# A gated cross-attention mix and a mixture of eight experts on one core: moving the first expert's weights into earlier tiles, a second early pair, and a shift made by ScalarE

## What is computed

```
si, sj = ctx @ Wi, ctx @ Wj                              # one number per row each
mix    = 0.6 * sigmoid(si[:, None] + sj[None, :] + b) + 0.4 * layernorm(x)
x      = x + tanh(g_xattn) * mix
h      = layernorm(x)
probs  = softmax(h @ wg)                                 # 8 experts
e      = argmax(probs)                                   # one expert per row
x      = x + tanh(g_ffn) * probs[e] * (h @ W[e].T + bias[e])
```

## Time and profile before

| | |
|---|---|
| time, median of 3 runs | 609.71 us (608.7 to 612.66) |
| the profiled execution | 609.34 us |
| its span, first to last instruction | 607.7 us |
| TensorE busy | 519.1 us (85%), mean granted clock 0.899 |
| VectorE busy | 405.6 us (67%) |
| POOL busy | 358.1 us (59%) |
| ScalarE busy | 292.5 us (48%) |

### The profile page before, as it was taken

One profiled execution on the slowest core, in us unless ns is written; L12 is line 12 of the kernel. 1 busy time (PEld: TensorE's weight loads), 2 busy tenths in 40 slices (PEclk: granted clock), 3 DMA queues, 4 the chain that ended last, 5 costly groups with the idle time before them and its releaser, 6 DMA issues.

```text
span 607.7 us, 14740 instructions
## 1 busy us (share of the span) xinstructions
PE 519.1 (85%) x2890; PEld 425.1 (70%) x2891; DVE 405.6 (67%) x538; ACT 292.5 (48%) x426; POOL 358.1 (59%) x537
## 2 busy tenths in 40 slices
PE   6467677675789994999999999999999999999980
PEld 5356566554568773887888888788888888878860
DVE  1867556999873775777777677777657757764330
ACT  3585565656423443454555445545454445453430
POOL 3696878775655551655556556456555564565652
PEclk9597777656679996999999999999999999999995
DMA  7952877997775775988988597798769857885530
GB/s 254 391 185 73 281 244 247 327 289 215 250 294 167 203 219 143 267 235 232 254 242 232 164 270 242 215 271 242 217 167 263 239 179 225 237 232 173 170 105 5
DMA packets 87755, 134.67 MB, mean 222 GB/s; under 512 B 11696, under 2 KB 69552, under 8 KB 87728
## 3 DMA queue, kind: packets, MB, share of 16 engines
q1 hardware_dynamic: 71504, 80.28, 48.0%
q0 software_dynamic: 15264, 54.06, 24.9%
q10 hardware_dynamic: 960, 0.00, 0.1%
HBM read 100.49 MB, written 35.91 MB: 224 GB/s over the span
## 4 chain that ended last, share of the span: by engine, by line
DVE 22%; issue 22%; POOL 16%; ACT 13%; PE 9%; ACTq 8%; DMA 3%; POOLq 3%; DVEq 1%; SPq 0%
DVE pair L917 5%; DVE xt L909 5%; ACT rb L710 5%; ACT xt L702 4%; PE pair L1146 4%; POOL scal L555 3%; POOL scal L558 3%; DVE raw L845 3%; DVE xr L856 3%; ACTq L780 2%; PE pair L1137 2%; DMA gates<-in_L_xattn_b 2%; POOL out_x L570 2%; ACTq L803 2%; PE pair L1158 1%
## 5 line engine op out<-in xcount | busy, mean ns | idle before, releaser
L1229 PE MATMUL pair<-wt,xt 128*128 (+1 forms) x1728 | 400.9, 394 | 14.2 <-DVE wt L925 14.0
L1229 PEld LDWEIGHTS pair<-wt,xt 128*128 128x128 f32 x1728 | 326.5, 189 | 88.3 <-issue 16.3
L909 DVE TENSOR_TENSOR xt<-pair,xt 128x1024 f32 (+1 forms) x38 | 46.5, 1225 | 67.4 <-ACT xt L702 67.4
L566 POOL TENSOR_TENSOR rows<-rows,rb 128x1024 f32<-128x1024 f32 x37 | 89.3, 2414 | 3.2 <-ACT rb L724 1.6
L696 ACT ACTIVATE wt<-pair 128x1024 f32 x54 | 55.5, 1028 | 58.1 <-DVE pair L917 54.7
L1146 PE MATMUL pair<-ident,xr 128*128 128x128 f32 x256 | 50.5, 362 | 36.4 <-DVE xr L856 36.4
L724 ACT ACTIVATE rb<-bias_bc,scal 128x1024 f32 (+1 forms) x37 | 46.0, 1245 | 71.7 <-POOL scal L562 71.7
L925 DVE TENSOR_TENSOR wt<-pair,wt 128x1024 f32 (+1 forms) x56 | 67.9, 1213 | 12.5 <-ACT wt L696 12.5
L1146 PEld LDWEIGHTS pair<-ident,xr 128*128 128x128 f32 x256 | 41.8, 193 | 44.0 <-DVE xr L856 34.3
L917 DVE STREAM_TRANSPOSE pair<-w_raw 128x1024 f32<-128x1024 f32 x56 | 69.4, 1240 | 3.6 <-DMA w_raw<-in_L_ffn_W 2.0
L570 POOL DMA_INDIRECT out_x<-rows,scatter_row x36 | 38.9, 1079 | 28.2 <-issue 26.8
(11 more groups left out here) (152 smaller groups left out, 416.4 us busy)
## 6 DMA issues: line engine op xcount, KB each, us to landing
w_raw<-in_L_ffn_W SPq DMA_DIRECT2D x264, 128.0 KB, 3.1
xb<-table SPq DMA_DIRECT2D x156, 128.0 KB
rows<-table POOLq DMA_DIRECT2D x38, 520.0 KB, 5.2
xr<-in_x SPq DMA_DIRECT2D x32, 512.0 KB, 7.8
ctx_in<-in_ctx SPq DMA_DIRECT2D x8, 512.0 KB, 6.1
bias_bc<-in_L_ffn_b SPq DMA_DIRECT2D x8, 512.0 KB, 6.5
out_x<-rows,scatter_row POOLq DMA_INDIRECT x36, 3.7
table<-xr,pos POOLq DMA_INDIRECT x32, 4.8
```

The costliest lines, as they stand in the source:

```text
L566: nc.gpsimd.tensor_tensor(rows[:, k, 0:H], rows[:, k, 0:H], rb[:, :], ALU.add).then_inc(base_ready, 1)
L909: nc.vector.tensor_tensor(xt[:, at, 1, :, :].rearrange("p a k n -> p (a k n)"), ps[:, :], xt[:, at, 0, :, :].rearrange("p a k n -> p (a k ...
L1229: last = nc.tensor.matmul(out_ps[r % 2][:, HALF * h:HALF * (h + 1)], xt[:, r % RING, x_part, k, :], wt[:, bass.ds(par, 1), w_part, k, HALF ...
```

## The change

The pieces of the first expert go beside tiles 6, 10, 14, 18, 20, 22, 24 and 26, and a piece's subtraction always to the tile behind. SP loads the first three pieces before the later contexts and tiles, the others behind tiles 18, 21, 24, 29 and 31. A piece that stands between contexts waits for the contexts begun before it, and TensorE's next context waits for the pieces cut before it, since both use `cut_a`. The first block of rows is turned at tile 28 instead of 29. The early part of the slots makes two pairs of the second expert instead of one, and the table counts them. POOL's shift (line 505) goes; ScalarE makes it in a new `shift(t)`, one tile behind its tanh, with a scale and a bias per partition, for which POOL negates `ln_ma` once per group.

```diff
-    WEIGHT_TILES = [18, 20, 21, 22, 24, 25, 26, 28]
-    ROW_TILES = [29, 31]
+    WEIGHT_TILES = [6, 10, 14, 18, 20, 22, 24, 26]
+    ROW_TILES = [28, 31]
+    EARLY_PAIRS = 2
+    PIECE_BEHIND = [18, 21, 24, 29, 31]
...
             sp.dma_start(bias_bc[:, 0, :], bias[0:1, :].to_broadcast([P, H])).then_inc(bias_landed, 16)
+            for m in range(WR):
+                load_piece(0, m)
             for g in range(4, 7):
                 next_context(g)
...
+                if t in PIECE_BEHIND:
+                    m = WR + PIECE_BEHIND.index(t)
                     sp.wait_ge(w_turned, m - WR + 1)
                     load_piece(0, m)
...
             sp.dma_start(bias_bc[:, 1, :], bias[1:2, :].to_broadcast([P, H])).then_inc(bias_landed, 16)
+            for n in range(2):
+                sp.wait_ge(w_turned, K + n + 1)
+                load_next(K + 2 + n, n)
...
             for n in range(2):
-                sp.wait_ge(w_turned, K + n + 1)
-                load_next(K + 2 + n, n)
+                sp.wait_ge(w_turned, K + 2 + n + 1)
+                load_next(K + 4 + n, n)
...
+                nc.gpsimd.tensor_scalar(ln_ma[:, four], ln_ma[:, four], -1.0, None, ALU.mult).then_inc(scales_of_tile, 1)
 
             def linear(t):
                 s = slot_of(t)
-                pool.wait_ge(th_ready, t + 1)
-                link(nc.gpsimd.tensor_scalar(ln_b[:, t:t + 1], xr[:, s, TH:TH + 1], nc2h[:, 0:1], ln_ma[:, t:t + 1],
-                                             ALU.mult, ALU.subtract))
+                pool.wait_ge(shift_ready, t + 1)
...
+            def shift(t):
+                act.wait_ge(th_ready, t + 1)
+                act.wait_ge(scales_of_tile, t // GR + 1)
+                nc.scalar.activation(ln_b[:, t:t + 1], xr[:, slot_of(t), TH:TH + 1], ACT.Identity,
+                                     scale=nc2h[:, 0:1], bias=ln_ma[:, t:t + 1]).then_inc(shift_ready, 1)
...
+            act.wait_ge(scales_ready, 1)
             for t in range(RTH - 1):
                 half_tanh(t)
+                if t:
+                    shift(t - 1)
             for t in range(T):
                 g, r = t // GR, t % GR
                 if t + RTH - 1 < T:
                     half_tanh(t + RTH - 1)
                 if r == 1 and g > 0:
                     logits_copy(g - 1)
+                if t + RTH - 2 < T:
+                    shift(t + RTH - 2)
                 copy_turned(t)
...
-            for u in range(EARLY):
-                square(u, u)
-                exp_sum(u, u)
-                scaled_bias(u, u, 0, 0)
-            xt_high(2, 2, cut_a)
+            square(0, 0)
+            exp_sum(0, 0)
+            scaled_bias(0, 0, 0, 0)
             for n in range(RX):
                 act.wait_ge(row_stored[n], 16 * (T // RX))
             for n, ps in enumerate((cut_b, cut_a)):
                 cut_high(1, n, 1, ps)
+            square(1, 1)
+            exp_sum(1, 1)
+            scaled_bias(1, 1, 0, 0)
+            xt_high(2, 2, cut_a)
+            for n, ps in enumerate((cut_b, cut_a)):
+                cut_high(1, 2 + n, 1, ps)
...
                 if t in WEIGHT_TILES:
-                    m = WEIGHT_TILES.index(t)
-                    if m:
-                        cut_low(0, m - 1, 0, cut_a)
-                    else:
-                        dve.wait_ge(si_ready, NG)
-                        dve.wait_ge(sj_ready, NG)
-                    turn_weights(0, m, cut_a)
+                    begun = len([n for n in range(2, NG) if ctx_turn_tile(n) < t])
+                    dve.wait_ge(si_ready, 2 + begun)
+                    dve.wait_ge(sj_ready, 2 + begun)
+                    turn_weights(0, WEIGHT_TILES.index(t), cut_a)
+                if t - 1 in WEIGHT_TILES:
+                    cut_low(0, WEIGHT_TILES.index(t - 1), 0, cut_a)
...
-            link(nc.vector.tensor_scalar(kinds[:, :], n_begun[:, :], 1.0, None, ALU.is_equal))
+            link(nc.vector.tensor_scalar(kinds[:, :], n_begun[:, :], 1.0, float(EARLY_PAIRS), ALU.is_equal, ALU.mult))
...
             nc.vector.tensor_tensor(slot_tab[:, 0, :], to_do[:, :], used[:, :], ALU.mult).then_inc(slots_told, 1)
+            dve.wait_ge(xt_ready, 2)
+            turn_pair(PAIRS, 0, cut_b)
+            turn_pair(PAIRS, 1, cut_a)
...
+            pair_low(PAIRS, 0, cut_b)
+            pair_low(PAIRS, 1, cut_a)
             finish(0, 0, 0, beyond_early[:, 0:1])
-            dve.wait_ge(xt_ready, 2)
+            dve.wait_ge(w_ready, K + 2)
             turn_rows(2, 1, 0, cut_a)
-            turn_pair(PAIRS, 0, cut_b)
+            turn_pair(PAIRS + 1, 0, cut_b)
             xt_low(2, 2, cut_a)
             dve.wait_ge(xt_ready, 3)
-            turn_pair(PAIRS, 1, cut_a)
-            pair_low(PAIRS, 0, cut_b)
-            pair_low(PAIRS, 1, cut_a)
-            settled(w_ready, K + 2)
+            turn_pair(PAIRS + 1, 1, cut_a)
+            pair_low(PAIRS + 1, 0, cut_b)
+            pair_low(PAIRS + 1, 1, cut_a)
+            settled(w_ready, K + 4)
...
                     pe.wait_ge(si_ready, 1 if g == 2 else g)
                     pe.wait_ge(sj_ready, 1 if g == 2 else g)
+                    lent = len([t for t in WEIGHT_TILES if t < ctx_turn_tile(g)])
+                    if lent:
+                        pe.wait_ge(w_ready, lent)
```

More of the change, by code:

```diff
@@ L225, in build @@
         lin_ready = sem("lin_ready")
+        scales_of_tile = sem("scales_of_tile")
+        shift_ready = sem("shift_ready")
         xc_ready = sem("xc_ready")
@@ L339, in _, with load_piece @@
             sp.dma_start(bias_bc[:, 0, :], bias[0:1, :].to_broadcast([P, H])).then_inc(bias_landed, 16)
+            def load_piece(e, m):
+                for q in (0, 2, 1, 3):
+                    sp.dma_start(w_raw[32 * q:32 * (q + 1), m % WR, :, :],
+                                 in_blocks(W[bass.ds(e, 1), P * m:P * (m + 1), :].rearrange("a o h -> (a o) h"),
+                                           q)).then_inc(w_landed[m % WR], 16)
+            for m in range(WR):
+                load_piece(0, m)
             for g in range(4, 7):
@@ L344, in _ @@
             next_context(7)
-            def load_piece(e, m):
-                for q in (0, 2, 1, 3):
-                    sp.dma_start(w_raw[32 * q:32 * (q + 1), m % WR, :, :],
-                                 in_blocks(W[bass.ds(e, 1), P * m:P * (m + 1), :].rearrange("a o h -> (a o) h"),
-                                           q)).then_inc(w_landed[m % WR], 16)
             for t in range(RX + 2, T):
                 next_tile(t)
-                if t == RX + 8:
-                    for m in range(WR):
-                        load_piece(0, m)
-                if t in (RX + 11, RX + 14, RX + 15):
-                    m = {RX + 11: 3, RX + 14: 4, RX + 15: 5}[t]
+                if t in PIECE_BEHIND:
+                    m = WR + PIECE_BEHIND.index(t)
                     sp.wait_ge(w_turned, m - WR + 1)
                     load_piece(0, m)
-            for m in range(6, K):
-                sp.wait_ge(w_turned, m - WR + 1)
-                load_piece(0, m)
             sp.wait_ge(th_ready, 3 * TB)
@@ L969, in _ @@
                 if t == ROW_TILES[0]:
-                    cut_low(0, K - 1, 0, cut_a)
                     dve.wait_ge(w_ready, K)
```

## The result

The changed kernel took **615.75 us** (median of 6 runs, 614.79 to 616.5) beside 609.62 us for the kernel before on the same chip (6 runs, 608.7 to 612.66). The ratio computed from the runs is 1.0075, interval 1.0055 to 1.0095; the two medians by themselves give 1.0101. So it is slower, by 4.6 us after the ratio and 6.1 us after the medians, where 604.6 us was forecast, 5 us faster than before. The profiled execution took 615.87 us, its span 614.2 us, mean granted clock 0.883 (before 609.34, 607.7 and 0.899).

What follows compares the result with a forecast made beforehand. TensorE bounds the experts, a chain of waits the early groups, VectorE the later ones. 609.34 + 1.4 opening + 3.9 pieces - 1.75 later tiles - 8.1 hole - 0.9 clock after it + 0.7 early clock = 604.6 us; range 598 to 613.2.

Steps and rivals of the forecast that it cites:

- TensorE's clock in the early groups: Early groups: longer waits can cost TensorE granted clock; 0.7 us added in all.
- TensorE's clock stays at 1.2 GHz in the early groups: Rival, early groups: low clock lengthens transposes and logits, 3.76 us a group with moved work, total 612.2 us; chance 0.16.
- a first product later than 183 us: Start of the expert products: T0 over 183 us would show the clock rival; the forecast had about 178 to 179.
- The reason held against it: Early groups, against the clock rival: TensorE's longest run, from the spread context to the route, stays.
- The moved work: Pieces at tiles 6, 10, 14: transpose 0.3 and subtraction 1.0 us a group, 3.9 us lost for three.
- The hole: Slot 4, TensorE waiting for the second expert's pairs: shrinks from 10.17 to about 2.05 us, 8.1 us gained.
- the cover that failed: Early slots: slot 2's rows, some 3 us later behind eight loads, stay hidden; if not, half of 8.1 us expected.
- The clock after the hole: Behind slot 4's hole: a shorter hole leaves TensorE's clock at 1.00, 0 to 1.45 us gained, 0.9 taken.
- The opening: Opening: ScalarE's shift delays copy_turned(2) and what queues behind it; 1.4 us lost, ends 0.5 and 2.5.
- Tiles 18 to 30: Later tiles: VectorE has 7.4 us less work, of which 1.75 us come out, ends 0.2 and 7.4.
- the moved loads were costed at nothing for the later contexts: SP: the first three pieces' loads ahead of context 4 may delay it, but it has slack: nothing, at worst 1 us.
- The sum: Whole kernel: all terms added to the profiled 609.34 us give 604.6 us; forecast's chance 0.48, own range 601 to 608.

Runs made afterwards that it cites:

- e4: The changed kernel with idle 512-column matmuls on TensorE from tile 6 on, nothing else changed: 602.98 us, ratio 0.989.
- e6: The changed kernel with the shift back on POOL and the idle matmuls on TensorE: 603.33 us, ratio 0.9866.
- e5: The kernel before with the two early pairs and the idle matmuls on TensorE: 598.78 us, ratio 0.9795.
- e3: The kernel before with the two early pairs of the second expert alone: 601.93 us, ratio 0.9854.
- e2: The kernel before with two early pairs and the shift on ScalarE, pieces and their loads left as before: 608.67 us, ratio 0.9964.
- e9: The changed kernel with idle matmuls in e4's places and number, but 8 columns wide instead of 512: 614.82 us, ratio 1.0077.
- e1: The changed kernel with the shift back on POOL: 613.5 us, ratio 1.0059.
- e8: The changed kernel with the shift on POOL and without VectorE's subtraction of the three early pieces: 606.18 us, ratio 0.9915.
- e7: The kernel before with two early pairs, SP fetching slot 2's rows ahead of the eight weight loads: 600.91 us, ratio 0.9823.
- e11: The kernel before with two early pairs, idle matmuls, and SP fetching slot 2's rows ahead of the eight loads: 598.79 us, ratio 0.9823.
- e12: The kernel before with the idle matmuls on TensorE alone: 606.9 us, ratio 0.9935.

## Why the prediction was wrong

**The step that failed is the choice made for TensorE's clock in the early groups**: forecast at 0.7 us in all, where 3.6 to 6.6 us were lost to it (worked out below), and, as the rival "TensorE's clock stays at 1.2 GHz in the early groups", given a chance of 0.16. That rival had its mechanism, its place and its size right: 3.76 us a group, where 10.75 / 3 = 3.58 were lost, and 612.2 us; what carries it to 615.9 stands below. The prediction's own sign for it, a first product later than 183 us, came too: 187.40. The reason held against it was that TensorE's longest run in a group stays. It does stay (66.70 to 71.94 before, 74.00 to 77.44 after, in the group shown), but the row that decides is not the longest run: it is which instructions the slow stretch falls on, and after the change it falls on tile 12, the context and the logits, for which choose waits. The earlier trace rows already had 0.77 in an early group; a stage at 0.77 has slow stretches, and they should have been followed row by row to what waits behind them. The Trainium skill, "TensorE: Matmul & The Clock Gate", section "HAM oscillation — how this bites in real kernels", tells, for a loop that waits for DMA, of waits between bursts that throttle the clock again and again; the early groups of the trace after, at 0.58 to 0.73 with waits for VectorE, agree with it, and e4 shows the price here, 11 to 13 us.

**The moved work.** The prediction took 1.3 us a group: 0.3 for the transpose, 1.0 for the subtraction. In the group shown above the add of tile 11 comes 0.32 us later against its group's first (6.96 after, 6.64 before) and tile 12's transposes 1.41 us: right, where the clock is left as it was. At a clock of 1.00 a piece costs more: a group with one takes 18.26 us in e4 and 18.29 in e6, one without 16.31 in e5. So 1.95 of the 2.48 us of VectorE's two instructions come through, and 0.5 stay hidden. The 10.75 us lost in the early groups divide differently by what is compared:

| compared | moved work | clock |
|---|---|---|
| the single group above, taken three times | 4.2 | 6.6 |
| groups at 1.00, three times 1.95 | 5.9 | 4.9 |
| all three groups, e4 against e5 (55.79 - 48.60) | 7.2 | 3.6 |

In the last row two of e4's groups stood at 0.91, so some clock is left in its 7.2. By each row the clock's 0.7 was far too small, and the 3.9 for the moved work too small as well, by 0.3 to 3.3 us. The rival's shares, 1.3 and 2.46 a group, are close to the 1.4 and 2.2 of the group shown; by the groups at 1.00 they are 1.95 and 1.6, so that its sum came so near is in part luck.

**The hole.** Forecast 10.17 to 2.05, measured 2.83. The new hole of 1.36 us ahead of slot 2 was the cover that failed: the rows of slot 2 were put "some 3 us later" and called hidden behind ScalarE's copy; they came 21.5 - 15.1 = 6.4 us later. The eight loads and the row that they go ahead of were seen, not how long SP takes to issue them and how late the rows then land. In sum -5.89 instead of -8.1. e3 says what this part is worth alone: 8.45 us, of 9.0 forecast for the hole and the clock behind it.

**The clock after the hole** is 1.00, as the forecast had it, but of its 0.9 us the 192 products behind the hole show 0.49 (45.06 us after, 45.55 before), and nothing reaches the end (-0.05 from the restart on). By the idle times on the pages the other holes behind the restart sum to 4.5 us, 3.9 before, which takes the 0.49.

**The opening.** Forecast +1.4, measured +1.51 from add 0 to add 6, by the mechanism named. The nearness is in part luck: with the shift on ScalarE the same stretch took 28.17 us in e2, 27.20 in e4 and 27.33 in e9, 2.35 to 3.3 more than before, and part of their TensorE rows there are slow. ScalarE's timeline after, the shift of tile 4 and copy_turned(2) behind it:

```profile
37.48 0.39 ACT L677 ACTIVATE ln_b<-xr,ln_ma,nc2h 128x1 f32<-128x1 f32 x1 [0.59 <-POOL ln_ma L504]
37.78 1.00 ACT L684 ACTIVATE xc_tr<-pair 128x1024 f32<-128x1024 f32 x1
```

A shift takes 0.38 us, and the next instruction starts 0.3 behind its start, against the 0.1 taken. The 1.34 us ahead of add 0 were not forecast: 13.57 - 12.51 = 1.06 of it is a small load of the gates that landed later, which the change doesn't touch.

**Tiles 18 to 30.** Forecast -1.75, measured -1.98.

**A step that came right for the wrong reason:** the moved loads were costed at nothing for the later contexts. In the kernel after TensorE waits for no context there; e1, e6 and e8 show waits of 3.45, 2.67 and 1.20 us with the shift gone. That is what came late next, and it is one reason why e1 gained so little. That the moved loads are what made the context late was not tried by itself.

**The sum.** By its own steps the forecast missed 615.87 - 604.6 = 11.3 us: 6.15 in the early groups (10.75 against 3.9 + 0.7), 2.2 in the slots, 0.85 behind the hole, 1.45 up to add 6, 0.8 between add 30 and the first product (clock 0.52 in that stretch after), less 0.2 in the later tiles. From the clock's rival it is 612.2 + 2.2 + 1.45 + 0.8 - 0.2, and less 0.55 for its 11.3 us where 10.75 were lost: 615.9. The range ended at 613.2, where the clock's rival with a late context had been put; the rival together with the slots' smaller gain lies outside it.

## What to carry to other kernels

Where a stage is bound by a chain of waits and the granted clock is below 1.00, an engine's idle time is no measure of what a moved instruction costs: follow TensorE's rows at either level to the one that the next wait hangs on, and price a shift of the slow stretch too. Before moving work into such a stage, try to hold the clock with idle matmuls into a bank that is overwritten anyway; here that gained some 4 us in the old order and 11 to 13 in the new, and told the clock's part of a price (7.0 of 11.6 us) from the moved work's. And time the parts of a change alone: one of the three gained 8.45 us and was hidden under two that cost some 13.5.

## What was not expected of the hardware

- A `tensor_scalar` of 48 columns, 0.25 us before, took 2.47 us at 198.48, where POOL's add of 1024 columns began at 198.50 and took 2.40. The Trainium skill, "SBUF — State Buffer", section "SBUF: two separate sides", says that VectorE, in its two-port modes or with two inputs in SBUF, and GpSimd lock each other out of a shared pair of ports for a whole instruction. The lengths of the two rows agree with it; in which mode VectorE ran here, no run shows. All that VectorE had queued behind it, the end of slot 0 (line 950) among it, came some 2.2 us later.
- The same instructions up to the first product gave 174.96 us in the kernel before and 175.66 in e7, 173.37 in e3; with the idle matmuls 170.58 in e5, 170.19 in e11 and 172.80 in e12. So the idle matmuls bring the first product sooner here, but not to a steadier time: the spread is 2.3 us without them and 2.6 with them.
